# A decoder layer on one core: the order of its first loads, its first tile in halves, and where a bias product stands

## What is computed

```
x = x + self_attention(layernorm(x), Wq, Wk, Wv, Wo)     # 32 query heads, 8 key heads of 16, rotary, causal
x = x + cross(layernorm(x), ctx, Wq', bq, Wk', bk)       # softmax((x Wq'^T + bq)(ctx Wk'^T + bk)^T / sqrt(512)) ctx
x = x + ffn(layernorm(x), gate, up, down)                # three ternary weights, inner width 1376
```

## Time and profile before

| | us |
|---|---|
| median of 3 runs | 226.55 (226.46 to 226.76) |
| the profiled execution, its time | 226.59 |
| its span in the profile | 224.8 |
| PE busy | 209.1 (93%) |
| PE weight loads | 151.8 (68%) |
| DVE busy | 147.7 (66%) |
| ACT busy | 124.9 (56%) |
| POOL busy | 65.8 (29%) |
| granted TensorE clock | 1.0 throughout |

### The profile page before, as it was taken

The page is one execution under the profiler, slowest core; times in us unless marked ns, Lnnn a source line. Parts: engine busy times, 40 slices in busy tenths (PEclk is TensorE's granted clock), DMA queues, the critical chain, the costliest instruction groups (busy, mean ns, idle before and its releaser), DMA issues.

```text
span 224.8 us, 4335 instructions
## 1 busy us (share of the span) xinstructions
PE 209.1 (93%) x1492; PEld 151.8 (68%) x1500; DVE 147.7 (66%) x556; ACT 124.9 (56%) x210; POOL 65.8 (29%) x87
## 2 busy tenths in 40 slices
PE   8799999999897899998999997999999999999993
PEld 3279878677664675565945545788887877767771
DVE  2488887977789875998524589886645665343333
ACT  2648788787988446196767917457325033323220
POOL 4499928694222383152202212000000010000000
PEclk9999999999999999999999999999999999999999
DMA  6999500024722310549100540000000000020002
GB/s 168 371 397 417 209 0 1 3 52 204 223 80 51 93 52 0 188 122 309 31 4 0 199 176 0 3 0 3 0 0 1 3 0 3 0 93 0 3 0 95
DMA packets 9078, 19.98 MB, mean 89 GB/s; under 512 B 1152, under 2 KB 1536, under 8 KB 9056
## 3 DMA queue, kind: packets, MB, share of 16 engines
q1 hardware_dynamic: 8480, 19.60, 25.0%
q10 hardware_dynamic: 576, 0.10, 0.2%
HBM read 18.58 MB, written 1.05 MB: 87 GB/s over the span
## 4 chain that ended last, share of the span: by engine, by line
PE 76%; DVE 7%; ACT 6%; issue 5%; DMA 3%; SPq 1%; DVEq 0%; POOL 0%; ACTq 0%
PE ps L1376 17%; PE ps L1230 13%; PE ps L1391 8%; PE ps L1267 5%; PE ps L1298 3%; PE ps L1329 3%; PE ps L1210 3%; DMA wqkv<-wqkv_dram 3%; PE ps L1439 3%; PE ps L1164 3%; PE ps L1521 3%; PE ps L1450 2%; PE ps L1480 2%; PE ps L1179 2%; PE ps L1189 2%
## 5 line engine op out<-in xcount | busy, mean ns | idle before, releaser
L1048 DVE CUSTOM_DVE_ANT_0 ps<-ps,maskf 128x128 f32<-128x128 f32 (+1 forms) x128 | 41.1, 394 | 3.1 <-PE ps L1450 2.1
L584 POOL TENSOR_SCALAR_AFFINE_SELECT prob<-prob 128x512 f32<-128x512 f32 x32 | 19.8, 643 | 49.0 <-ACT prob L802 48.9
L802 ACT ACTIVATE prob<-ps 128x1536 f32<-128x1536 f32 x16 | 23.3, 1454 | 19.3 <-PE ps L1486 19.3
L503 POOL TENSOR_TENSOR rstd<-veps,neghalf 128x1 f32<-128x1 f32 x12 | 7.3, 609 | 58.3 <-DVE veps L837 58.3
L672 ACT CAST in_hi<-inter 128x256 f16<-128x256 f32 (+1 forms) x22 | 8.9, 405 | 23.1 <-DVE inter L1001 23.1
L1376 PE MATMUL ps<-h_hi,gate_q 128*128 128x256 f16 (+1 forms) x88 | 20.5, 273 | 0.0
L1376 PE MATMUL ps<-h_lo,up_q 128*128 128x256 f16 (+1 forms) x88 | 20.4, 273 | 0.0
L1376 PE MATMUL ps<-h_hi,up_q 128*128 128x256 f16 (+1 forms) x88 | 20.4, 273 | 0.0
L1376 PE MATMUL ps<-h_lo,gate_q 128*128 128x256 f16 (+1 forms) x88 | 20.4, 272 | 0.0
L1001 DVE TENSOR_TENSOR inter<-gate_s,ps 128x256 f32<-128x256 f32 (+1 forms) x22 | 9.2, 418 | 15.6 <-PE ps L1376 14.7
L665 ACT ACTIVATE gate_s<-ps 128x256 f32<-128x256 f32 (+1 forms) x22 | 8.4, 384 | 18.8 <-PE ps L1376 18.8
(11 more groups left out here) (189 smaller groups left out, 540.2 us busy)
## 6 DMA issues: line engine op xcount, KB each, us to landing
raw<-gate_dram SPq DMA_DIRECT2D x1, 2752.0 KB, 17.1
raw<-up_dram SPq DMA_DIRECT2D x4, 688.0 KB, 4.4
wqkv<-wqkv_dram SPq DMA_DIRECT2D x4, 384.0 KB, 6.3
raw<-down_dram SPq DMA_DIRECT2D x2, 768.0 KB, 5.2
x<-x_dram SPq DMA_DIRECT2D x4, 256.0 KB, 5.8
xwq<-xwq_dram SPq DMA_DIRECT2D x1, 1024.0 KB, 9.1
xwk<-xwk_dram SPq DMA_DIRECT2D x1, 1024.0 KB, 11.1
wo<-wo_dram SPq DMA_DIRECT2D x1, 1024.0 KB, 18.7
```

What stands on the lines that cost most here:

```text
L584: nc.gpsimd.affine_select(out=v, in_=v, compare_op=ALU.is_ge, fill=0.0, base=0, pattern=[[0, GROUP], [1, P]], channel_multiplier=-1).then_ ...
L802: nc.scalar.activation(prob[:, i % 2, :], ps[:, 3:6, :].rearrange("p a b -> p (a b)"), ACT.Exp, scale=DH ** -0.5).then_inc(exp_done, 1)
L1048: nc.vector.tensor_tensor_reduce(scores, scores, mask, 1.0, LOWEST, ALU.add, ALU.max, to).then_inc(max_done, 1)
```

## The change

Four edits, made together:

1. The four small tables are no longer issued by ACT. SP issues `rope` between w2 and w3, and the mask and the biases after x3. Among the large loads w1 now goes before x1, and x2 after w3. `rope` gets a semaphore of its own.
2. Tile 0 is normalised in two halves of 256 features, each half transposed into a bank of its own and copied by an ACT instruction of its own; ACT rounds w0 before these copies. PE projects tile 0 part by part, both groups of columns for each part; `tile_T(1)` now stands between part 1 and part 2.
3. The rest of the early order follows: POOL does each `w_low` ahead of the root beside it, ACT copies transposed tile 1 before it rounds w3.
4. The bias product and `fold` move from DVE's early part to the step that holds `("c",)`, behind `("out", 7)` and ahead of the wait for PE's column product.

```diff
@@ sync: loads
             for k in range(KD):
                 sp.dma_start(wqkv[:, k, :], wqkv_d[k * P:(k + 1) * P, :]).then_inc(wqkv_in[k], 16)
-                if k < 2:
-                    load_x(1 + k)
+                if k == 1:
+                    load_x(1)
+                if k == 2:
+                    sp.dma_start(rope[:, :, :, :], rope_d).then_inc(rope_in, 16)
+            load_x(2)
             load_x(3)
+            sp.dma_start(maskf[:, P:2 * P], mask_d).then_inc(const_in, 16)
+            sp.dma_start(bqk[:, 0, :], bq_d).then_inc(const_in, 16)
+            sp.dma_start(bqk[:, 1, :], bk_d).then_inc(const_in, 16)
@@ gpsimd
+            w_low(0)
             root(1)
-            w_low(0)
+            w_low(1)
             root(2)
-            w_low(1)
+            w_low(2)
             pool.wait_ge(xn_ready, 2)
             root(3)
-            w_low(2)
             w_low(3)
-            pool.wait_ge(const_in, 16 * 4)
+            pool.wait_ge(const_in, 16 * 3)
+            pool.wait_ge(rope_in, 16)
@@ scalar
-            act.dma_start(rope[:, :, :, :], rope_d).then_inc(const_in, 16)
-            act.dma_start(maskf[:, P:2 * P], mask_d).then_inc(const_in, 16)
-            act.dma_start(bqk[:, 0, :], bq_d).then_inc(const_in, 16)
-            act.dma_start(bqk[:, 1, :], bk_d).then_inc(const_in, 16)
+            def first_T():
+                for half, full, done in ((0, xnT_half_ps, xnT_half), (1, xnT_ps, xnT_sb)):
+                    act.wait_ge(full, 1)
+                    nc.scalar.copy(xnT[:, 2 * half:2 * half + 2, 0:P],
+                                   bank(FIRST_BANKS[half], T).rearrange("p (k q) -> p k q", k=2)).then_inc(done, 1)
...
-            tile_T(0)
             weights_high(0)
+            first_T()
             weights_high(1)
             normalise(1)
             weights_high(2)
+            tile_T(1)
             weights_high(3)
             normalise(2)
-            tile_T(1)
@@ vector
-                    normalise(0, lambda: None)
+                    dve.wait_ge(rstd_ready, 1)
+                    for half, ready in ((0, xn_half), (1, xn_ready)):
+                        cols = slice(half * T, (half + 1) * T)
+                        nc.vector.tensor_scalar(xn[:, 0, cols], x[:, 0, cols], mv[:, 0, 0:1], rstd[:, 0:1],
+                                                ALU.subtract, ALU.mult).then_inc(ready, 1)
...
-            dve.wait_ge(const_in, 16 * 4)
+            dve.wait_ge(rope_in, 16)
...
-            nc.vector.tensor_tensor_reduce(stat[:, 0, 0:KD], bqk[:, 0, :], bqk[:, 1, :], 1.0, 0.0,
-                                           ALU.mult, ALU.add, dotp[:, :]).then_inc(dot_ready, 1)
...
-            link(nc.vector.tensor_reduce(fold[:, :], ident[:, :].rearrange("p (j r) -> p r j", r=32), AX.X, ALU.add))
...
                     elif kind == "c":
+                        dve.wait_ge(const_in, 16 * 3)
+                        nc.vector.tensor_tensor_reduce(xmx[:, 0:KD], bqk[:, 0, :], bqk[:, 1, :], 1.0, 0.0,
+                                                       ALU.mult, ALU.add, dotp[:, :]).then_inc(dot_ready, 1)
+                        link(nc.vector.tensor_reduce(fold[:, :], ident[:, :].rearrange("p (j r) -> p r j", r=32),
+                                                     AX.X, ALU.add))
                         wait_side(dve, *piece)
@@ tensor
+            def first_T():
+                for half, ready, full in ((0, xn_half, xnT_half_ps), (1, xn_ready, xnT_ps)):
+                    pe.wait_ge(ready, 1)
+                    for j in range(2):
+                        k = 2 * half + j
+                        mm = nc.tensor.transpose(bank(FIRST_BANKS[half])[:, j * P:(j + 1) * P],
+                                                 xn[:, 0, k * P:(k + 1) * P], ident[:, :])
+                    mm.then_inc(full, 1)
+            def project_first(k):
+                pe.wait_ge(xnT_sb if k >= 2 else xnT_half, 1)
+                pe.wait_ge(wqkv_in[k], 16)
+                for e in range(2):
+                    mm = nc.tensor.matmul(qkv_bank(0, e)[:, 0:QKV - D if e else D], xnT[:, k, 0:P],
+                                          wqkv[:, k, HEAD_COLS[e]], start=(k == 0), stop=(k == KD - 1))
+                    if k == KD - 1:
+                        mm.then_inc(qkv_ps, 1)
...
-            tile_T(0)
-            pe.wait_ge(xnT_sb, 1)
-            project_first(qkv_bank(0, 0), 0).then_inc(qkv_ps, 1)
-            tile_T(1)
-            project_first(qkv_bank(0, 1)[:, 0:QKV - D], 1).then_inc(qkv_ps, 1)
+            first_T()
+            for k in range(KD):
+                if k == 2:
+                    tile_T(1)
+                project_first(k)
             project_high(qkv_bank(1, 0), 1, 0)
```

More of the change, by code:

```diff
@@ L171, in decoder_layer @@
         x_in = [sem(f"x_in{t}") for t in range(TT)]
-        ident_in = sem("ident_in")
+        ident_in, rope_in = sem("ident_in"), sem("rope_in")
         wqkv_in = [sem(f"wqkv_in{k}") for k in range(KD)]
@@ L185, in decoder_layer @@
         xnT_ps, xnT_sb, xnT_low = sem("xnT_ps"), sem("xnT_sb"), sem("xnT_low")
+        xn_half, xnT_half_ps, xnT_half = sem("xn_half"), sem("xnT_half_ps"), sem("xnT_half")
         w_high, w_low_done = sem("w_high"), sem("w_low_done")
@@ L211, in bank @@
             return ps[:, n, 0:width]
-        TILE_BANK = (0, 5, 6, 0)
+        TILE_BANK = (None, 5, 6, 0)
+        FIRST_BANKS = (0, 6)
         ST_BANKS = (5, 1, 6, 2)
@@ L592, in _ @@
         def _(act):
-            act.dma_start(rope[:, :, :, :], rope_d).then_inc(const_in, 16)
-            act.dma_start(maskf[:, P:2 * P], mask_d).then_inc(const_in, 16)
-            act.dma_start(bqk[:, 0, :], bq_d).then_inc(const_in, 16)
-            act.dma_start(bqk[:, 1, :], bk_d).then_inc(const_in, 16)
             def tile_T(t):
                 act.wait_ge(xnT_ps, t + 1)
-                nc.scalar.copy((xnT if t == 0 else xnT_r)[:, :, t * P:(t + 1) * P],
+                nc.scalar.copy(xnT_r[:, :, t * P:(t + 1) * P],
                                bank(TILE_BANK[t]).rearrange("p (k q) -> p k q", k=KD)).then_inc(xnT_sb, 1)
+            def first_T():
[3 more added lines that the diff above has]
+                                   bank(FIRST_BANKS[half], T).rearrange("p (k q) -> p k q", k=2)).then_inc(done, 1)
             def heads_high(t, e):
@@ L1168, in tile_T @@
                 pe.wait_ge(xn_ready, t + 1)
+                if t == 2:
+                    pe.wait_ge(xnT_sb, 1)
                 if t == 3:
-                    pe.wait_ge(xnT_sb, 1)
+                    pe.wait_ge(xnT_half, 1)
                 transpose_tile(bank(TILE_BANK[t]), xn[:, t % 2, :]).then_inc(xnT_ps, 1)
             HEAD_COLS = (slice(0, D), slice(D, QKV))
-            def project_first(out, e):
-                for k in range(KD):
-                    pe.wait_ge(wqkv_in[k], 16)
-                    mm = nc.tensor.matmul(out, xnT[:, k, 0:P], wqkv[:, k, HEAD_COLS[e]],
-                                          start=(k == 0), stop=(k == KD - 1))
-                return mm
+            def first_T():
[14 more added lines that the diff above has]
+                        mm.then_inc(qkv_ps, 1)
             def project_high(out, t, e):
```

## The result

| | us |
|---|---|
| after, median of 20 runs | 227.15 (226.16 to 228.16) |
| before, on the same chip, median of 20 runs | 226.63 (226.03 to 227.21) |
| ratio | 1.0022, 95% interval 1.0012 to 1.0033 |
| the profiled execution, its time | 227.58 |
| its span | 225.9 (before 224.8) |

The change is slower by 0.5 us (0.3 to 0.7).

A forecast was written before the change was run, and what follows sets the result against it. Taken to bound the kernel: the front up to tile 1's rounded product at 14.24 us, through weight loads and PE, with DVE's path equally long. Front -1.0 and step 11 +0.1 give -0.9, 226.59 to 225.7 us; range 225.0 to 227.0.

The forecast's parts named there:

- g = 1.8: First loads: x1 lands 1.8 us sooner with the tables out of the way, 1.0 bandwidth and the rest skew.
- The price of the order: First loads: w1 ahead of x1 makes x1 land 0.97 us later.
- L + 6.35: Front: DVE's low part of tile 1 is ready 6.35 us after x1's landing, the later path to the rounded product.
- The bound of -1.6: Front: with everything landed early, tile 1's rounded product starts at 12.55, so at most 1.6 us is gained.
- Halves 0: Front, tile 0: normalising, transposing and copying it in two halves earns 0 by itself.
- Bias product and fold +0.1 at step 11: Step 11: the moved instructions cost DVE 0.25 us, the span 0.1; freeing DVE early counts 0.
- POOL's low part of w0 ... no later than today's: Front, POOL: the low part of w0 and its followers come no later than 9.34.
- (a): Rival, first loads: slow stretch not the tables', landing gain only 0.3 to 0.8 us; time 226.8; chance 0.22.
- (b): Rival, front: DVE's second half of tile 0 stands behind POOL's rounding-off of w0; time 226.5; chance 0.17.
- (c): Rival, step 11: bias product slow by itself, 1.17 us, adding 1.1 to the span; chance 0.11.
- (d): Rival: product slow on first use, so the first row maximum pays 1.0 us; time 226.0; chance 0.07.
- (e): Rival: the clock falls because PE idles about 0.4 us before tile 1's transposes; chance 0.03.

The follow-up runs named there:

- e2: Kernel before with edit 1 alone (small tables late on SP, w1 before x1, x2 behind w3): +1.1 us against the kernel before.
- e5: Kernel before with only the two bias loads moved to SP behind x3: -0.6 us against the kernel before.
- e7: e3 with tile 0 normalised, transposed and copied whole, still projected part by part: -0.3 us against the kernel before.
- e4: Kernel after with all four small tables issued by ACT again, large loads left as changed: +0.7 us against the kernel before.
- e11: Kernel before with only the changed order of large loads (w1 before x1, x2 behind w3): +0.8 us against the kernel before.
- e12: Kernel after with x1 ahead of w1 again, x2 still behind w3: +1.0 us against the kernel before.
- e1: Kernel before with edit 4 alone (bias product and fold moved to step 11): 226.58 us beside 226.55, change 0.0.
- e14: e3 run again in another batch: -0.2 us against the kernel before.
- e17: Kernel before with edits 2 to 4, but POOL's old order kept, and the identity loaded behind w0: -0.6 us against the kernel before.
- e6: e3 with the identity loaded behind w0: -0.8 us against the kernel before.
- e9: e3 with the identity loaded behind x3, and rope, mask and biases after it: run once, 232.35 us.
- e15: Kernel before with edits 2 to 4, identity behind w0, POOL's root of tile 1 ahead of its first low part: +1.2 us against the kernel before.
- e3: Kernel after with large loads in their old order (x1 ahead of w1, x2 ahead of w2), tables still last: -0.4 us against the kernel before.
- e10: Kernel before with edits 2 to 4 and the two bias loads moved to SP behind x3: -0.4 us against the kernel before.

## Why the prediction was wrong, step by step

**The step that failed** is "g = 1.8": the landing L of x1 was given as 8.60 - g, with the slow stretch of the earlier trace rows put down to the tables. Measured: L = 8.51, g = 0.1. The prediction put g together from 1.0 of bandwidth and 0.8 of engines out of step. The bandwidth gave 0.4 to 0.5 (x1's middle part, the bytes on SP's queue). The other part gave nothing: the last part of x1 came 0.3 further behind the middle than before. e2, with the same loads, landed x1 at 7.75, g = 0.85, so the size of g is only known as 0.1 to 0.9; no trace shows 1.8 in this order. e5 has the stretch without the small packets of the biases, at 195 GB/s; after, e2 and e7 have it without any table, one large load earlier. The reading of the earlier trace rows was right in size (1 us lost) and wrong in owner. "The small ones can only be the biases" was right too, and beside the point: that packets share a stretch with a slow transfer doesn't say that they slow it. The same view could have warned. Of the engines' time the small packets' queue had 4.7%, and SP's 73.3%; the line of the kernel before beside those of the earlier trace rows, queue, packets, MB and share:

```profile
q10 hardware_dynamic: 84, 0.00, 4.7%
```

By the Trainium skill (DMA: Bandwidth & Descriptors, Issuing engines are not separate DMA queues) another issuing engine only saves the time of issuing. No run here shows that alone, since the move to SP also put the tables later: after and e4 differ by the move and land x1 at 8.51 and 8.55, but e2 and e11 differ by the same move and land it at 7.75 and 8.81. For what the prediction took from that page of the Trainium skill for the biases' packets e5's stretch gives no support.

**The price of the order** was known and right: w1 ahead of x1 +0.97 (e11: 1.18). What was not seen is that x2's place alone is enough to lose the gain. "x2 lands L + 2.6, the low part is ready at L + 2.6 + 3.75" stood in the prediction (measured 2.77 and 3.58; 1056 KB are 1.08 MB, which makes 2.66), and so DVE's path was known to be the later one; but both terms hung on L, so that a failed g took the whole with it. A bound with g applied to x1 alone would have shown it, and e12 is that case: x1 at 6.22, and no gain left in the median.

**Path model.** L + 6.35 gives 14.86 for the measured L; the product started at 14.98. With the measured L the steps give +0.6 at the front and up to +0.1 at step 11; the medians show +0.5, the two profiled executions +1.0. "What both paths gain before 14.24 should stay" was right, one for one in 17 profiles. The bound of -1.6 is -1.7 by its own terms (12.55 - 14.24), without effect on the forecast.

**Halves 0**: right as far as can be told (e7). **Bias product and fold +0.1 at step 11**: right within what can be told (e1: 0.0, by its interval -0.3 to +0.3; in the traces 0.08 on DVE for the 0.25 forecast, and nothing on PE); that DVE had stood behind POOL is borne out, 0.15 for 1.17. **"POOL's low part of w0 ... no later than today's"**: right in itself, but the step never asked what is queued behind it. The root of tile 1 is, and e14 against e17 shows that it starts 0.9 late as soon as x1 lands near 6.5. So even with x1 at the forecast 6.8 the product would have started near e14's 13.44, 0.8 earlier than before, not 1.1.

**Rivals.** (a) is what happened: g small, and the stretch not the tables'. Its g of 0.3 to 0.8 fits the bytes (0.4 to 0.5) and e2's landing, not the landing in after (0.1). Its price (+0.3, 226.8) fell short by 0.2 as a difference (0.35 as a time), at the edge of the measured 0.3 to 0.7. (b) did not occur in the kernel after, but is shown by e6 and e9 (with the first half held, not the second), and gone in e15 and e17, where POOL does the root first. The Trainium skill (SBUF — State Buffer, Who interferes with whom), by which a DVE tensor_scalar contends with GpSimd as well, agrees with e6: 2.30 us beside POOL's 1.82, 0.73 without. (c) and (d) fell with 0.15 and 0.29. (e): the clock stayed at 1.0.

**The chances.** Slower by over 0.2% had 0.17, faster 0.50. The half for "faster" rested on one untested reading, and (a) had 0.22 with most of it put into "within 0.2%", by a g that again counted a gain for the tables. The measured time lies 0.15 above the range.

## What to carry to other kernels

When a slow stretch of the queues coincides with small transfers, look at whose time it is: if the small ones take a few per cent of the engines' time, move one of them before counting on the stretch. In a front written out by hand, price a moved load by its last user in each engine's own order: x2 was needed "late" for tile 2's products, and early for tile 1, since DVE does its statistics first. And before a long instruction is moved up on an engine, ask which short one is behind it and who waits for that: 0.55 us of root behind 1.8 or 3.6 us of low part delayed it by 0.9 and by 2.2 (DVE's 2.87 less its usual 0.67). And before a landing is read out of one trace, look at a second trace with the same loads: here they differed by up to 0.8 us.

## What the runs showed of the hardware that was not expected

At the start of the loads there is a hole worth up to about 1 us, at its deepest 170 to 196 GB/s between stretches of 347 to 408 (after, e2, e3, e7; before, e5), flatter in other traces. It moves with the order of the small loads; in the one kernel that had no small load ahead of the large ones (e9) none of the three stretches from 3 to 8.5 us was below 334 GB/s. The 16 parts of one load drift apart: x1's last part came 0.3 to 1.3 us behind its middle one in before, after, e1, e5 and e10, and the waiting engine starts with the last. DVE's tensor_scalar on 128x256 is held up by a POOL tensor_tensor on SBUF until that instruction ends (1.98 and 1.89 us in e6 and e9, 0.41 otherwise), as a 4-column product was (1.17 against 0.15).
